# Attention in pairs of cores: one output bank and one close for two, scores 14 steps ahead, a third score bank

## What is computed

```
x_norm = modulate(_ln(x), shift_a, scale_a)
q, k, v = jnp.split(x_norm @ W_qkv + b_qkv, 3, axis=-1)          # to (B, 16, 128, 8)
attn_w = softmax(einsum('bhqd,bhkd->bhqk', q, k) * 8 ** -0.5)
x = x + gate_a * (einsum('bhqk,bhkd->bhqd', attn_w, v) @ W_proj + b_proj)
q_c = _ln(x) @ W_qc + b_qc
k_c, v_c = jnp.split(_ln(context) @ W_kvc + b_kvc, 2, axis=-1)
x = x + softmax(q_c k_c * scale) v_c @ W_cproj + b_cproj
x_norm2 = modulate(_ln(x), shift_m, scale_m)
x = x + gate_m * (gelu(x_norm2 @ W_mlp1 + b_mlp1) @ W_mlp2 + b_mlp2)
# then, per token: LayerNorm, a softmax over keys from the context ("evidence"),
# a router over 3 experts, a gate, and x + g * (routed @ out_w + out_b)
```

## Time and profile before

| | |
|---|---|
| median of 3 runs | 693.39 us (688.67 to 694.4) |
| profiled execution | 692.35 us, span 690.6 us, mean granted PE clock 0.989 |
| PE matmul busy | 603.5 us, 87% of the span |
| DVE busy | 471.8 us, 68% |
| ACT busy | 406.3 us, 59% |
| POOL busy | 217.7 us, 32% |
| first score, first exp, last exp | 36.0 us, 51.5 us, 419.7 us |

### The profile page before, as it was taken

The page is one execution under the profiler, slowest core; times in us unless marked ns, Lnnn a source line. Parts: engine busy times, 40 slices in busy tenths (PEclk is TensorE's granted clock), DMA queues, the critical chain, the costliest instruction groups (busy, mean ns, idle before and its releaser), DMA issues.

```text
span 690.6 us, 18075 instructions
## 1 busy us (share of the span) xinstructions
PE 603.5 (87%) x6281; PEld 393.9 (57%) x6281; DVE 471.8 (68%) x1393; ACT 406.3 (59%) x985; POOL 217.7 (32%) x232
## 2 busy tenths in 40 slices
PE   0668987989889988998888997999799999999996
PEld 0334553555555545555445664445468877887885
DVE  3167887888888888788779754354457567656654
ACT  0226675677676676776666766444555466547653
POOL 7334343234244352352443401012222322232110
PEclk9999999999999999999999999999999999999998
DMA  9412332333333233222332200000000010010000
GB/s 307 109 48 75 82 86 52 81 90 78 78 86 79 72 78 84 78 75 64 101 76 62 61 3 15 17 0 0 17 0 19 30 31 17 15 30 16 16 16 17
DMA packets 72948, 39.03 MB, mean 57 GB/s; under 512 B 8921, under 2 KB 72506, under 8 KB 72762
## 3 DMA queue, kind: packets, MB, share of 16 engines
q1 hardware_dynamic: 68232, 33.47, 18.5%
q10 hardware_dynamic: 4658, 4.81, 2.2%
HBM read 9.93 MB, written 2.10 MB: 17 GB/s over the span
## 4 chain that ended last, share of the span: by engine, by line
PE 55%; DVE 19%; ACT 9%; issue 7%; POOL 4%; ACTq 2%; SPq 1%; DMA 1%; DVEq 1%; POOLq 0%
PE PS L847 26%; PE PS L1610 6%; DVE NM L1399 5%; PE PS L1564 5%; PE PS L1539 5%; PE PS L884 2%; PE PS L1622 2%; PE PS L1584 2%; PE PS L1606 2%; ACTq L1276 2%; DVE stat L1454 2%; DVE rest L1493 2%; PE PS L1551 1%; POOL XN L1248 1%; POOL XN L1251 1%
## 5 line engine op out<-in xcount | busy, mean ns | idle before, releaser
L1304 ACT ACTIVATE PR<-PS 128x512 f32<-128x512 f32 x256 | 153.6, 601 | 75.5 <-PE PS L1551 67.8
L1399 DVE TENSOR_REDUCE NM<-PS 128x4 f32<-128x512 f32 x256 | 171.6, 682 | 29.8 <-PE PS L1539 29.1
L1539 PE MATMUL PS<-Ks,Qs 64*128 64x128 bf16 x1024 | 102.9, 224 | 20.2 <-DVE NM L1399 14.2
L1564 PE MATMUL PS<-PR,Va 128*32 128x128 f32 x2048 | 109.5, 286 | 0.1
L1551 PE MATMUL PS<-Qs,Ks 64*128 64x128 bf16 x1024 | 101.8, 220 | 0.6 <-ACT PR L1304 0.6
L1539 PEld LDWEIGHTS PS<-Ks,Qs 64*128 64x128 bf16 x1024 | 58.1, 96 | 76.9 <-DVE NM L1399 40.4
L658 ACT ACTIVATE r_HID<-PS,ANC 128x128 f32<-128x128 f32 x224 | 63.2, 370 | 43.3 <-PE PS L847 43.3
L1551 PEld LDWEIGHTS PS<-Qs,Ks 64*128 64x128 bf16 x1024 | 57.8, 95 | 2.3 <-issue 1.3
L847 PE MATMUL PS<-r_NXS,r_WNS 128*128 128x512 f32 x168 | 54.1, 430 | 5.6 <-ACT r_HID L658 5.6
L1564 PEld LDWEIGHTS PS<-PR,Va 128*32 128x32 f32 x2048 | 40.5, 108 | 27.1 <-issue 0.6
L1258 POOL TENSOR_TENSOR Qp<-rest,zeros 128x512 bf16<-128x512 f32 x16 | 20.3, 1267 | 102.1 <-DVE rest L1493 102.1
(11 more groups left out here) (177 smaller groups left out, 1122.0 us busy)
## 6 DMA issues: line engine op xcount, KB each, us to landing
Qs<-Qp SPq DMA_DIRECT2D x168, 64.0 KB
Ks<-Kp SPq DMA_DIRECT2D x168, 64.0 KB
W<-in_weights ACTq DMA_DIRECT2D x1, 2564.5 KB
X<-in_x ACTq DMA_DIRECT2D x8, 256.0 KB, 7.2
CTXG<-in_ctx SPq DMA_DIRECT2D x8, 256.0 KB, 3.3
r_CTX<-in_ctx SPq DMA_DIRECT2D x8, 256.0 KB, 2.9
out<-X SPq DMA_DIRECT2D x8, 256.0 KB, 2.3
Qs<-Qp SPq DMA_DIRECT2D x12, 128.0 KB
```

The costliest lines, as they stand in the source:

```text
L1304: nc.scalar.activation(PR[:, u, :], T_BANK[u % 2][:, :], ACT.Exp, scale=SCALE)\
L1399: nc.vector.tensor_reduce(out=NM[:, r, 4 * u:4 * u + 4], in_=S_BANK[u % 2][:, :].rearrange("p (h k) -> p h k", k=P), axis=AX.X, op=ALU.max ...
L1539: last = nc.tensor.matmul(S_BANK[u % 2][:, j * P:(j + 1) * P], Qs[c.mem][rows, lo + j, cols], Ks[c.mem][rows, lo + j, cols], start=True, s ...
L1564: last = nc.tensor.matmul(O_BANK[c.mod % 2][32 * j:32 * j + 32, u * P:(u + 1) * P], Va[c.mem][:, c.b, 4 * u + j, :], PR[:, u, j * P:(j + 1 ...
```

## The change

**Pairs.** Two neighbouring cores of a `mem` make a `Pair` (32 in all, four in an iteration, eight steps each). `Va` is laid out in 64 columns per two heads, so that a value step u = 0 or 2 writes a head to rows 0 to 15 of each 32-row strip, and the step u = 1 or 3, with columns shifted by 16 and accumulation on, adds the next head in rows 16 to 31 of the same columns. A core now takes 256 columns of an `O_BANK` and a pair fills it. The close (`OTs` copy, *o_turn*, *o_norm*, *o_back*, `OgT` copy) is done once for the pair, with operands twice as wide in *o_norm*, *o_back* (two transposes) and `OgT`; *max_parts* and *max_turn* are done once too, for both cores (two small transposes, one copy, two DMAs). Columns of the value weights and rows of the output projections are permuted on the host to match.

**Banks.** *max_turn* and *o_back* now write into the pair's `O_BANK`, and `SMALL_BANK` (bank 7) becomes a third `S_BANK`. `score_bank` gives the bank of a step and how many steps back it was used last (3, at the wrap of an iteration 2 or 5).

**Lead.** Scores go 14 steps (`LEAD`) ahead of *shifted*, before 10. In iterations 0, 1 and 7 the scores of steps t = 2 to 9 are put off by `LATE_SCORES`: none at t = 2 to 4, two each at 5, 6 and 7. All places of fills, statistics and stack DMAs are set anew, and one iteration less is in the loop.

```diff
-VW = 32
+VW = 64
+TW = 32
+LEAD = 14
...
+def score_bank(c, u):
+
+    t = (4 * (4 * c.mem + c.b) + u) % 32
+    return t % 3 if t < 30 else t - 30, {0: 2, 1: 2, 2: 5}.get(t, 3)
...
 def regular_steps(i):
...
+            + fill_steps(1.2, "xt_s", i + 2, (0, 1.3), (1, 1.4))
+            + fill_steps(3.9, "q0", i + 1, (0, 4.0), (1, 4.4))
+            + fill_steps(5.9, "k0", i + 1, (0, 6.0), (1, 6.4))
...
+            + fill_steps(24.5, "proj_s", i + 1, (0, 24.8), (1, 24.9))
+            + fill_steps(26.0, "yt_s", i + 1, (1, 26.4)))
...
+    for h in range(2):
+        own = moves("zero", h) + moves("Q", h) + moves("K", h)
+        steps += [(8 + 8 * h + 0.5 * k, 0, i + 1, *m, (i, 2 * h + 1)) for k, m in enumerate(own)]
...
+LATE_SCORES = {2: (), 3: (), 4: (), 5: (16, 17), 6: (18, 19), 7: (20, 21), 8: (22,), 9: (23,)}
...
 def attention_events(i, steady=False):
...
+            if w == 2 and ahead1:
+                yield ("max_parts", ahead1)
+            early = not steady and i in (0, NG - 2) and p == 2
+            if w == (4 if early else 5) and back1:
+                yield ("o_turn", back1, back1.n + 1 + bool(here) + bool(ahead1))
+                yield ("o_norm", back1)
+            if w == (5 if early else 7) and back1:
+                yield ("o_back", back1)
+            yield from group_steps(t, t + 0.5)
+
+            late = LATE_SCORES.get(t) if not steady and i in (0, 1, NG - 1) else None
+            for ahead in (LEAD,) if late is None else (x - t for x in late):
+                c, u = core(ahead)
+                if c:
+                    yield ("score", c, u)
+            for name, ahead in (("shifted", 0), ("value", -2)):
+                c, u = core(ahead)
+                if c:
+                    yield (name, c, u)
+            if w == 3 and ahead1:
+                yield ("max_turn", ahead1, ahead1.n - bool(here))
+            yield from group_steps(t + 0.5, t + 1)
...
-        S_BANK, T_BANK, O_BANK, GROUP_BANK, SMALL_BANK = PS[0:2], PS[2:4], PS[4:6], PS[6], PS[7]
+        S_BANK, T_BANK, O_BANK, GROUP_BANK = (PS[0], PS[1], PS[7]), PS[2:4], PS[4:6], PS[6]
...
-                    if not isinstance(c.n, int) or 4 * c.n + u > 1:
-                        pe.wait_ge(max_done, 4 * c.n + (u - 1))
+                    bank, ago = score_bank(c, u)
+                    if not isinstance(c.n, int) or 4 * c.n + u >= ago:
+                        pe.wait_ge(max_done, 4 * c.n + (u + 1 - ago))
...
                 elif name == "value":
...
-                            pe.wait_ge(o_normed, c.n - 1)
+                            pe.wait_ge(o_stored, p.n - 1)
+                        pe.wait_ge(max_copied, p.n + 1)
...
+                    at = (2 * c.second + u // 2) * P
                     for j in range(4):
-                        last = nc.tensor.matmul(O_BANK[c.mod % 2][32 * j:32 * j + 32, u * P:(u + 1) * P],
-                                                Va[c.mem][:, c.b, 4 * u + j, :], PR[:, u, j * P:(j + 1) * P],
-                                                start=True, stop=True)
+                        last = nc.tensor.matmul(O_BANK[p.turn][TW * j:TW * j + TW, at:at + P],
+                                                Va[c.mem][:, c.b, 4 * (u // 2) + j, u % 2 * TW // 2:u % 2 * TW // 2 + TW],
+                                                PR[:, u, j * P:(j + 1) * P], start=u % 2 == 0, stop=u % 2 == 1)
                     last.then_inc(value_done, 1)
                 elif name == "max_turn":
-                    _, c, stored = ev
+                    _, c, copied = ev
                     pe.wait_ge(max_parts, c.n + 1)
...
+                        pe.wait_ge(o_copied, copied)
```

## The result

| | before | after |
|---|---|---|
| median (15 executions each, same chip) | 693.15 us | 698.50 us |
| profiled execution, span | 692.35, 690.6 us | 696.92, 694.9 us |
| mean granted PE clock of the profiled execution | 0.989 | 0.963 |

The ratio of after to before is 1.0077, 95% interval 1.0045 to 1.0109. I had forecast 661 us, 4.7% less. The changed kernel is 0.8% slower.

The account below looks back on a forecast made before the run. PE was taken as the bound, busy 91% in the loop. 692.35 - 24 (work removed) - 19 (idle time) + 3.8 + 4.8 + 2 + 1 (added costs) gave 661 us, range 655 to 671, and 649 to 683 with rivals.

Parts of the forecast that it names:

- the clock: PE's granted clock: one fall at the start stall, perhaps one saved elsewhere; 0 with 2 us either way.
- PE work removed: Pair closes on PE: 19.2 us fewer o_turn and 4.8 us fewer o_back transposes, 24 us gained.
- Rival C: Close of a pair exposed, PE waiting for ACT at max_turn and o_turn: 744 us, 703 with one handover; chance 0.06.
- PE idle time: Attention, 60 to 420 us: PE's idle 36.7 us falls to 17.6, 2.2 an iteration; 19 us gained.
- The third bank: Scores in the loop: nearly all of PE's 1.6 us an iteration of waits for DVE's reduces should go.
- Written-out iterations: Iterations outside the loop: their stalling more than the loop ones was named as a way to be wrong.
- What is added: Costs outside the loop: start +3.8, put-off scores 4.8, SP after the bursts +2, end +1 us.
- The stall at the start: First mem 1 score waits for DMAs issued behind the maxima, until 61.9 us: +3.8 us (0 to 6).
- The put-off scores: Iterations 0, 1 and 7: score groups beside one of their own half cost 1.6 us each, 4.8 us.
- Rival B: SP's DMA issues become the bound in the loop, 43 us an iteration: 683 us; chance 0.17.
- A: Rival: more PE idle time goes, 1.0 us idle and 39.1 us an iteration: 651 us; chance 0.20.
- rival D: No change within 1%: transposes not on the path, third bank only moves the wait; about 690 us; chance 0.07.

Follow-up runs that it names:

- s8: The changed kernel with the four transposes of o_turn done twice in each pair: 706.24 us, 1.0187 of the kernel before.
- s4: The changed kernel with two score banks instead of three: 707.84 us, 1.0221 of the kernel before.
- s3: The changed kernel with mem 1's first stack and first context load issued ahead of the maxima, plus unread matmuls at the start: 0.9962 of the kernel before.
- s10: s3 with iteration 1's ln_x statistics ahead of ln_s's instead of behind: 685.63 us, 0.9854 of the kernel before.
- s11: s10 without the put-off of scores in iteration 0: 0.9872 of the kernel before.
- s18_best_scored: s10 with iteration 7's seven derive fills at steps 4.4 to 17.4, all but the last ahead of the last score: 689.01 us, 0.9843 of the kernel before.
- s5: s3 plus 128 unread matmuls ahead of six fills in iterations 0, 1, 6 and 7: 0.9969 of the kernel before.
- s16: The changed kernel with iteration 7's seven derive fills spread from step 4.4 to 20.9: 686.22 us, 0.9873 of the kernel before.
- s13: s10 with iteration 7's seven derive fills spread from step 4.4 to 20.9: 0.9884 of the kernel before.
- s1: The changed kernel with mem 1's first stack, ones and first context load issued ahead of the maxima: 1.0007 of the kernel before.
- s14: s10 without the unread matmuls at the start: 0.9951 of the kernel before.
- s17: The changed kernel with iteration 7's seven derive fills at steps 4.4 to 17.4, all but the last ahead of the last score: 695.34 us, 1.0016.
- s7: s3 with ln_x normalised later in iterations 0, 1 and 6, and xt_x and q1 later in 0 and 6: 0.9955 of the kernel before.

## Why the prediction was wrong

**The step that failed first is the clock, put at 0 with 2 us either way. It is the largest error: 11.6 us by the fit, and 4.4 at the start that the clock column misses.** I had one row of a fall and priced one stall at the start. I did not ask how often an engine at 95% would stop for a microsecond, nor how long a fall lasts: 17 us in iteration 7. The rule of the Trainium skill that I had cited spoke against the change, and I used it for one stall only.

**PE work removed, 24 us: oversized.** The count (76 transposes in 200 us, 0.28 each) was right. The error was to take all of it as path. By s8, 14 us of such work cost 7.6, with an interval of some 4 us either way; at that rate the 19.2 us of *o_turn* were worth about 10. Part of the rest covered the wait of *o_back* for `On`, a handover that I had called hidden. Rival C had a close exposed, but at *max_turn* and *o_turn* behind ACT, which shows one wait of 0.5 us in the whole attention; the one that came is 4.5 us over 19 pairs, 0.24 a pair, where C needed 1 to turn the sign.

**PE idle time, 19 us.** The third bank is worth 10 us (s4), where 1.6 us in eight iterations made 13. `XN` in the loop went and `YT` grew as worked out. PE was busy 95% from 200 to 300 us, though 10 of these 100 us were at the half clock. Iterations 3 to 5 took 41.0 to 41.8 us where I gave 40 to 41, iteration 2 43.7. The loop was forecast nearly right (42.0 us on average for 40.3); what failed was to multiply it by eight.

**Written-out iterations.** Named as a way to be wrong, and not priced. Iteration 1's 3.24 us behind DVE's order is worth 7.5 us with what follows it (s3 against s10). Iteration 0 took 8.2 us more than before: the stall and the half clock behind it are 6.9 by the trace of s3, and a wait of 1.8 us for `XN` near its end is new. Iterations 6 and 7 took 48.4 and 45.1.

**What is added.** The stall at the start was right in kind. SP's last issue ended at 60.51 for 59.9, and the first score of `mem` 1 (t = 5) came at 63.47 for 62. Undone, it gave 4.9 us, and 2.4 in the trace, for +3.8. Step t = 6, forecast at 63.2, began at 67.42, for a projection of 2.08 us at the half clock stands before it, which I had not counted. My own terms made 62.6 there (61.9 and one step), not 63.2. The put-off scores, 1.6 us an iteration, showed nothing in iteration 0 (s11). The value step with accumulation is no longer (290 ns mean from 150 to 350 us, as little as before), as I took it. Rival B is not settled. It asked for SP issuing without pause, which nearly came (6.2 us of pauses in 168), and for waits that end in DMA landings, of which PE has only 1.8 us in 200. With 37.8 us of issues in an iteration of 42, SP leaves little room for the 40.3 forecast, let alone for A. A run with fewer issues would tell. The time lies where rival D had it, within 1%, but not for D's reason: the third bank did more than move a wait (s4), and PE waits for DVE's reduces only 2.1 us in 200.

From the forecast of 661 to 698.5 are 37 us. The clock 11.6 and 4.4, the transposes 9, the third bank 3 and iteration 1's stall 3.2 make 31; some 6 stay open, in iterations 6 and 7 and in SP's part of the loop. Most of these terms are known only to 4 us and they overlap (s4 and s8 contain some clock of their own), so the sum shows that the order of size is right and no more. Open as well is what decides in a given execution whether the clock falls in iteration 7, and why fillers did not bring it back. No run held the clock.

s10_order_1 beats both kernels: 0.985 of the kernel before, 15 us under the changed one. s18_best_scored reached the lowest times of all (678.7 us), but not in most executions.

## What to carry to other kernels

Work taken off the busiest engine is worth only what of it did not stand in a wait: look which handover or which queue the removed instructions were covering, and double them to learn their price. An engine that only issues DMAs belongs in that look: count its pauses before and after. A gain per loop iteration must be checked against every iteration that is written out apart, in the order of each engine's queue. A PE that is busier but stops for a microsecond here and there can lose more to its clock than the schedule gives.

## What the runs showed of the hardware

- The granted clock fell behind gaps well under the 3.4 us stall: in s5 after waits of 0.80 and 0.43 us. Stretches alike to a few hundredths were followed by full clock in s16 and by half in s13. In the six executions of s16 the mean clock went from 0.987 to 0.960 and the time with it, from 684 to 698 us.
- At the start of the changed kernel the granted clock is shown as 1.00 while a pair of fp32 matmuls of 128x512 takes 2.08 us, until 72.9 us; it takes 1.12 at full speed later on. There the durations tell the clock, the column does not. The half speed there cost 4.4 us (73.68 for 78.11 us in s3 and s1, 72.75 for 77.19 in s10 and s14).
- Once fallen in iteration 7, the clock stayed at half for 14 us (s11) to 34 us (s17, 396 to 430 us) with PE busy nearly without a break.
- DVE's normalisation of four blocks took 1.11 us in the changed kernel, where GpSimd stood still, and 3.02 in s7 (from 123.81 us), where GpSimd worked on the key parts from 123.74 to 126.23.
- A DMA issue took SP 0.6 us, and 61 of them an iteration left it 6.2 us of pauses in 168 us of the changed kernel's loop.
